# Residual kept by channel through the first two attention layers of a four-layer image kernel: one load of the image, softmax divided ahead of its transpose, no transposes ahead of the group norms

## What is computed

```python
# L0: attention over max-pooled keys, 256 tokens x 64 pooled keys
theta = x @ w_theta + b_theta;  phi, g = maxpool2x2(x @ w_phi + b_phi), maxpool2x2(x @ w_g + b_g)
x = x + sigma * (softmax(theta @ phi.T) @ g @ w_o + b_o)
# L1: group norm (32 groups), one head of 128 channels, 256 x 256 scores
n = group_norm(x) * gamma + beta
x = x + softmax(q(n) @ k(n).T / sqrt(128)) @ v(n) @ wo + bo
# L2: group norm (16 groups), 8 heads of 16 channels
x = x + concat_heads(softmax(q @ k.T / 4) @ v) @ w_out + b_out
# L3: two 2-D Hartley transforms around a block-diagonal two-layer MLP with a soft threshold
x = x + dht2d(soft_threshold(mlp(dht2d(x)))) / (16 * 128)
```

## Time and profile before

| what | value |
|---|---|
| median of 3 runs | 162.05 us (162.05 to 164.85) |
| the profiled execution, its own time | 161.73 us |
| its span, first to last instruction | 159.9 us |
| PE busy | 152.9 us, 96% of the span |
| DVE busy | 102.3 us, 64% |
| ACT busy | 106.7 us, 67% |
| POOL busy | 53.1 us, 33% |
| HBM read, written | 4.08 MB, 1.05 MB |

### The profile page before, as it was taken

The page is one execution under the profiler, slowest core; times in us unless marked ns, Lnnn a source line. Parts: engine busy times, 40 slices in busy tenths (PEclk is TensorE's granted clock), DMA queues, the critical chain, the costliest instruction groups (busy, mean ns, idle before and its releaser), DMA issues.

```text
span 159.9 us, 3806 instructions
## 1 busy us (share of the span) xinstructions
PE 152.9 (96%) x1437; PEld 117.0 (73%) x1437; DVE 102.3 (64%) x257; ACT 106.7 (67%) x245; POOL 53.1 (33%) x128
## 2 busy tenths in 40 slices
PE   7999999998999999999999999999999999999992
PEld 4787978877877767977576867567577675668992
DVE  0448778888978677658986656747685571225543
ACT  3669668757287656877357776675856778776970
POOL 6566886624802632643001125022004000024300
PEclk9999999999999999999999999999999999999999
DMA  5996000000000000000000000000002001000003
GB/s 151 239 365 264 6 2 0 2 4 0 0 0 8 0 0 4 4 0 4 0 4 6 4 0 4 3 7 0 0 3 75 0 4 37 0 4 0 21 16 131
DMA packets 3233, 5.50 MB, mean 34 GB/s; under 512 B 400, under 2 KB 2320, under 8 KB 3216
## 3 DMA queue, kind: packets, MB, share of 16 engines
q1 hardware_dynamic: 2928, 5.05, 9.5%
q10 hardware_dynamic: 288, 0.21, 0.4%
HBM read 4.08 MB, written 1.05 MB: 32 GB/s over the span
## 4 chain that ended last, share of the span: by engine, by line
PE 85%; DMA 4%; ACT 3%; DVE 2%; POOL 2%; issue 1%; SPq 1%; DVEq 0%
PE psum L692 11%; PE psum L703 10%; PE psum L671 9%; PE psum L619 5%; PE psum L599 5%; DMA tab<-in_weights 4%; PE psum L744 3%; PE psum L730 3%; PE psum L773 3%; PE psum L647 3%; PE psum L581 2%; PE psum L714 2%; PE psum L655 2%; PE psum L590 2%; PE psum L765 2%; PE psum L766 2%
## 5 line engine op out<-in xcount | busy, mean ns | idle before, releaser
L1181 DVE TENSOR_REDUCE nmax<-psum 128x4 f32<-128x1024 f32 x32 | 38.1, 1218 | 12.2 <-PE psum L671 12.1
L954 ACT ACTIVATE pT<-psum 128x1024 f32<-128x1024 f32 x32 | 31.7, 1022 | 9.1 <-PE psum L692 9.0
L692 PE MATMUL psum<-qk 32*128 32x256 f32 (+1 forms) x256 | 18.3, 400 | 0.3 <-ACT vaug_all L941 0.3
L671 PE MATMUL psum<-qk 16*128 16x256 f32 (+1 forms) x256 | 18.1, 397 | 0.3 <-ACT vaug_all L941 0.3
L703 PE MATMUL psum<-pT,vaug_all 128*32 128x256 f32 x256 | 17.1, 385 | 0.0
L365 POOL COPY zE<-zE 128x17 f32<-128x17 f32 x8 | 1.6, 199 | 40.6 <-ACT zE L970 40.6
L671 PEld LDWEIGHTS psum<-qk 16*128 16x128 f32 (+1 forms) x256 | 11.7, 184 | 4.5 <-issue 1.2
L692 PEld LDWEIGHTS psum<-qk 32*128 32x128 f32 (+1 forms) x256 | 11.6, 184 | 4.0 <-DVE nmax L1181 1.1
L429 POOL TENSOR_SCALAR nb<-nmax,e 128x1 f32<-128x1 f32 x16 | 5.8, 373 | 25.7 <-DVE nmax L1156 24.9
L359 POOL TENSOR_TENSOR rstd<-vare,half 128x1 f32<-128x1 f32 x16 | 8.8, 558 | 8.2 <-DVE vare L1139 8.1
L703 PEld LDWEIGHTS psum<-pT,vaug_all 128*32 128x32 f32 x256 | 6.7, 109 | 6.3 <-issue 2.0
(11 more groups left out here) (163 smaller groups left out, 352.7 us busy)
## 6 DMA issues: line engine op xcount, KB each, us to landing
out<-x SPq DMA_DIRECT2D x8, 128.0 KB, 2.0
tab<-in_weights SPq DMA_DIRECT2D x1, 708.0 KB, 9.5
tab<-in_weights SPq DMA_DIRECT2D x1, 640.0 KB, 5.7
x0T<-in_xT SPq DMA_DIRECT2D x4, 128.0 KB, 3.1
xin<-in_x SPq DMA_DIRECT2D x2, 256.0 KB, 7.4
x0T<-in_xT_rest SPq DMA_DIRECT2D x1, 512.0 KB, 7.7
xin<-in_x SPq DMA_DIRECT2D x1, 512.0 KB, 8.7
tab<-in_weights SPq DMA_DIRECT2D x1, 384.0 KB, 8.4
```

Of the source, the lines that this page charges most:

```text
L671: last = mm(bank[(b0, b1)[j // 2] + j % 2][:, u * TOK:(u + 1) * TOK], at[:, u, 0, :], at[:, :, 1, :], start=True, stop=True)
L692: last = mm(bank[(b0, b1)[j // 2] + j % 2][:, m * TOK:(m + 1) * TOK], at[:, m, 1, :], at[:, :, 0, :], start=True, stop=True)
L954: go(pT[g](i)[:, 2 * k:2 * k + 2].rearrange("p j m t -> p j (m t)"), pair(home["st", g, i][k]), ACT.Exp).then_inc(s["exp" + "EO"[g]], 1)
L1181: v.tensor_reduce(nmax2(i)[:, g, 2 * k:2 * k + 2, :], pair(home["sm", g, i][k]).rearrange("p j (u m) -> p j u m", u=TILES), AX.X, ALU.max, ...
```

## The change

The residual now stays by channel in `x0T` through L0 and L1, and no image by token is loaded. The steps that differ:

- `o0` and `o1` have their operands swapped, so that the output comes by channel: `o0` is two products of 128 columns (one of 258 before), `o1` two of 256 (four of 129 before). There is no column of sums any more; the division must come before the transpose, since behind it the sum of a token is spread over a row. DVE sums `p0` (`sum0_out`), takes the reciprocal, and multiplies `p0` by it in place (`p0_scaled`, 128x128). For L1, `exp1` returns the row sums itself (`accum_out`), and `p1_scaled` (128x512) divides. `p0t` and `p1t` wait for these.
- `x1_out` and `x2_out` are one instruction of 256 columns each, in place on `x0T`. `x1t` and `x1b_out` are gone. Moments and normalisation read `x0T` in SBUF instead of a transposed copy in PSUM.
- `x2t` remains, but runs late, right ahead of `ont`, into the other half of `ont`'s bank; `onc` copies both halves (512 columns instead of 256), and `x3_out` takes the residual from there. `x2b_out` writes a tile of its own.
- Two folded biases are columns of one element in place of rows of 128.
- All five lists of calls are new.

```diff
-        x0T_all, xin_all = sb("x0T", [P, IMAGES, TOK]), sb("xin", [P, IMAGES, TILES, C])
+
...
-            load_tokens(0, 2)
             load_rest()
-            load_tokens(2, 2)
-            load_tokens(4, 4)
             load_table(sp.dma_start, 3)
             load_table(sp.dma_start, 4)
...
-            def x1b_out(i, *marks):
-                after(marks)
-                if i == 0:
-                    pool.wait_ge(s["vo_rd"], 1)
-                pool.wait_ge(s["x1"], i + 1)
-                gp.tensor_tensor(x1b(i), x1(i), wide(bo1_wide[:, :]), ALU.add).then_inc(s["x1b"], 1)
-
             def x2b_out(i, *marks):
                 after(marks)
                 if i == 0:
                     pool.wait_ge(s["o2_rd"], 1)
                 pool.wait_ge(s["x2"], i + 1)
-                gp.tensor_tensor(x2b(i), x2(i), wide(b_out2[:, :]), ALU.add).then_inc(s["x2b"], 1)
+                gp.tensor_scalar(x2b(i), x0T(i), b_out2[:, :], None, ALU.add).then_inc(s["x2b"], 1)
...
-                pe.wait_ge(s["wide_b2"], 1)
-                mm(bank[b][:, 0:C], bv2_wide[:, :], w("w2_o"), start=True, stop=True).then_inc(s["fold_o2"], 1)
+                pe.wait_ge(s["b2_rd"], 1)
+                mm(bank[b][:, 0:1], w("w2_o"), bv2[:, :], start=True, stop=True).then_inc(s["fold_o2"], 1)
...
-                pe.wait_ge(s["p0"], i + 1)
+                pe.wait_ge(s["p0n"], i + 1)
...
-                mm(bank[b][:, 0:TILES * (C + 1)], p0T(i), gw_all[:, i % SLOTS].rearrange("p u c -> p (u c)"),
-                   start=True, stop=True).then_inc(s["o0"], 1)
-
-            def x1t(i, b, *marks):
-                freed(*marks)
-                home["x1t", i] = b
-                pe.wait_ge(s["x1"], i + 1)
-                for u in range(TILES):
-                    last = tr(bank[b][:, u * P:(u + 1) * P], x1(i)[:, u, :], ident)
-                last.then_inc(s["x1T"], 1)
+                for u in range(TILES):
+                    last = mm(bank[b][:, u * P:(u + 1) * P], gw_all[:, i % SLOTS, u, :], p0T(i), start=True, stop=True)
+                last.then_inc(s["o0"], 1)
...
-                mm(bank[home["x1t", i]][:, TOK:TOK + 2], w("mean1"), mv[0](i), start=True, stop=True).then_inc(s["gm1"], 1)
+                mm(bank[home["o0", i]][:, TOK:TOK + 2], w("mean1"), mv[0](i), start=True, stop=True).then_inc(s["gm1"], 1)
...
-                pe.wait_ge(s["p1"], i + 1)
+                pe.wait_ge(s["p1n"], i + 1)
...
-                for u in range(TILES):
-                    for m in range(TILES):
-                        last = mm(bank[b][:, u * (C + 1):(u + 1) * (C + 1)], p1T(i)[:, m, u * P:(u + 1) * P],
-                                  v1_all[:, i % SLOTS, m, :], start=(m == 0), stop=(m == TILES - 1))
+                for m in range(TILES):
+                    last = mm(bank[b][:, 0:TOK], v1_all[:, i % SLOTS, m, :], p1T(i)[:, m, :],
+                              start=(m == 0), stop=(m == TILES - 1))
                 last.then_inc(s["o1"], 1)
 
             def x2t(i, b, *marks):
+
                 freed(*marks)
                 home["x2t", i] = b
-                pe.wait_ge(s["x2"], i + 1)
-                for u in range(TILES):
-                    last = tr(bank[b][:, u * P:(u + 1) * P], x2(i)[:, u, :], ident)
+                pe.wait_ge(s["x2b"], i + 1)
+                for u in range(TILES):
+                    last = tr(bank[b][:, TOK + u * P:TOK + (u + 1) * P], x2b(i)[:, u * P:(u + 1) * P], ident)
...
-                    last = tr(bank[b][:, u * P:(u + 1) * P], on(i)[:, u].rearrange("p h d -> p (h d)"), ident)
+                    last = tr(bank[home["x2t", i]][:, u * P:(u + 1) * P], on(i)[:, u].rearrange("p h d -> p (h d)"), ident)
...
-                              bias=nb1(i)[:, u:u + 1])
+                              bias=nb1(i)[:, u:u + 1], accum_out=sum1(i)[:, u:u + 1])
...
-                copy(onT(i), bank[home["ont", i]][:, 0:TOK]).then_inc(s["onT"], 1)
+                copy(onT(i), bank[home["x2t", i]][:, :]).then_inc(s["onT"], 1)
...
+            def sum0_out(i, *marks):
+                after(marks)
+                dve.wait_ge(s["p0"], i + 1)
+                v.tensor_reduce(sum0(i), p0(i), AX.X, ALU.add).then_inc(s["sum0"], 1)
+
             def inv0_out(i, *marks):
                 after(marks)
+                dve.wait_ge(s["sum0"], i + 1)
+                v.reciprocal(inv0(i), sum0(i)).then_inc(s["inv0"], 1)
+
+            def p0_scaled(i, *marks):
+
+                after(marks)
+                dve.wait_ge(s["inv0"], i + 1)
+                v.tensor_tensor(p0(i), p0(i), inv0(i).unsqueeze(2).to_broadcast((P, TILES, POOLED)), ALU.mult
+                                ).then_inc(s["p0n"], 1)
+
+            def x1_out(i, *marks):
+
+                after(marks)
                 dve.wait_ge(s["o0"], i + 1)
-                sums = bank[home["o0", i]][:, 0:TILES * (C + 1)].rearrange("p (u c) -> p u c", u=TILES)[:, :, C]
-                v.reciprocal(inv0(i), sums).then_inc(s["inv0"], 1)
-
-            def x1_out(i, *marks):
-                after(marks)
-                dve.wait_ge(with_xin(i), 16)
-                dve.wait_ge(s["inv0"], i + 1)
-                for u in range(TILES):
-                    last = v.scalar_tensor_tensor(out=x1(i)[:, u, :], in0=bank[home["o0", i]][:, u * (C + 1):u * (C + 1) + C],
-                                                  scalar=inv0(i)[:, u:u + 1], in1=xin(i)[:, u, :],
-                                                  op0=ALU.mult, op1=ALU.add)
-                last.then_inc(s["x1"], 1)
+                v.tensor_tensor(x0T(i), bank[home["o0", i]][:, 0:TOK], x0T(i), ALU.add).then_inc(s["x1"], 1)
 
 
 
             def moments(i, layer, *marks):
                 after(marks)
-                dve.wait_ge(s[f"x{layer}T"], i + 1)
-                v.bn_stats(bn[layer - 1](i), bank[home[f"x{layer}t", i]][:, 0:TOK]).then_inc(s[f"bn{layer}"], 1)
+                dve.wait_ge(s[f"x{layer}"], i + 1)
+                v.bn_stats(bn[layer - 1](i), x0T(i)).then_inc(s[f"bn{layer}"], 1)
 
             def mean(i, layer, *marks):
                 after(marks)
...
-                g = bank[home[f"x{layer}t", i]][:, TOK:TOK + 2]
+                g = bank[home[f"o{layer - 1}", i]][:, TOK:TOK + 2]
...
-                x = bank[home[f"x{layer}t", i]]
-                v.tensor_scalar(xn[k](i), x[:, 0:TOK], x[:, TOK:TOK + 1], rstd[k](i), ALU.subtract, ALU.mult
+                mean_of_group = bank[home[f"o{k}", i]][:, TOK:TOK + 1]
+                v.tensor_scalar(xn[k](i), x0T(i), mean_of_group, rstd[k](i), ALU.subtract, ALU.mult
...
+                dve.wait_ge(s["p1"], i + 1)
+                v.reciprocal(inv1(i), sum1(i)).then_inc(s["inv1"], 1)
+
+            def p1_scaled(i, *marks):
+
+                after(marks)
+                dve.wait_ge(s["inv1"], i + 1)
+                v.tensor_tensor(p1(i), p1(i), inv1(i).unsqueeze(2).to_broadcast((P, TILES, TOK)), ALU.mult
+                                ).then_inc(s["p1n"], 1)
+
+            def x2_out(i, *marks):
+                after(marks)
+                if i == 0:
+                    dve.wait_ge(s["vo_rd"], 1)
+                dve.wait_ge(s["x1"], i + 1)
                 dve.wait_ge(s["o1"], i + 1)
-                sums = bank[home["o1", i]][:, 0:TILES * (C + 1)].rearrange("p (u c) -> p u c", u=TILES)[:, :, C]
-                v.reciprocal(inv1(i), sums).then_inc(s["inv1"], 1)
-
-            def x2_out(i, *marks):
-                after(marks)
-                dve.wait_ge(s["x1b"], i + 1)
-                dve.wait_ge(s["inv1"], i + 1)
-                for u in range(TILES):
-                    last = v.scalar_tensor_tensor(out=x2(i)[:, u, :], in0=bank[home["o1", i]][:, u * (C + 1):u * (C + 1) + C],
-                                                  scalar=inv1(i)[:, u:u + 1], in1=x1b(i)[:, u, :],
-                                                  op0=ALU.mult, op1=ALU.add)
-                last.then_inc(s["x2"], 1)
...
-                dve.wait_ge(s["x2b"], i + 1)
                 dve.wait_ge(s["o2"], i + 1)
-                v.tensor_tensor(x3(i).rearrange("p u c -> p (u c)"), bank[home["o2", i]][:, 0:TOK],
-                                x2b(i).rearrange("p u c -> p (u c)"), ALU.add).then_inc(s["x3"], 1)
+                v.tensor_tensor(x3(i).rearrange("p u c -> p (u c)"), bank[home["o2", i]][:, 0:TOK], onT(i)[:, TOK:2 * TOK],
+                                ALU.add).then_inc(s["x3"], 1)
 
...
-            keep_clock(11, 7); proj0(0, 0); proj0(1, 1); proj0(2, 2); proj0(3, 0, ("theta", 1))
-            s0(0, 1, ("theta", 2)); gwm(0, 3); gwm(1, 4); gwm(2, 5); s0(1, 2, ("theta", 3)); s0(2, 6); p0t(0, 1)
...
+            keep_clock(11, 7); proj0(0, 0); proj0(1, 1); proj0(2, 2); s0(0, 0); proj0(3, 3); s0(1, 1); gwm(0, 4)
+            gwm(1, 5); gwm(2, 0, ("p0", 1)); p0t(0, 2, ("theta", 3)); fold_biases(6); o0(0, 2); s0(2, 1, ("p0", 2))
```

342 lines of the change are left out of this document (161 added, 181 removed).

## The result

The kernel after took 159.53 us (median of 4, 159.26 to 159.84), against 162.05 before: a ratio of 0.985, 95% interval 0.983 to 0.987. That is 1.5% less, inside the 2% line; forecast were 158.6 and a range of 156.0 to 162.8, with more weight on faster by over 2% (0.48) than on what came (0.38).

The account below looks back on a forecast made before the run. PE, busy 96% of the span, was taken to set the time, with room on the others. The sum 161.73 - 3.2 - 0.4 + 0.3 gave 158.4, told as 158.6 us for the median; range 156.0 to 162.8.

Parts of the forecast that it names:

- PE, -3.2: PE's matmul work: 1.8 us less by `x1t`, 1.4 less by `o1`, nothing by `o0`; sum -3.2 us.
- mis-sized at 1.4: `o1` on PE: four instructions of 256 columns at 0.86 us replace 1.0 an image; 0.17 saved each, 1.4 us.
- the 1.8 of `x1t`: PE loses two transposes an image, 0.22 us, times 8: 1.8 us saved.
- The start, -0.4: Up to the first `qk1`: 1.4 us earlier, less 1.0 of moved work; 0.4 us gained, bounds 0 to 1.4.
- the group means should come near 11: At the start: image 0's group means, at 13.18 us before, should come near 11.
- What this costs PE: PE's waits from added work on DVE and ACT: +0.3 us, upper bound 3.
- DVE, +5.9 or 3.8: DVE's added work: 0.74 us an image, 5.9 in all; a faster `normalised` would take back 2.1.
- PE's share of the chain stays over 80%: Sign to check in the profile after: PE keeps over 80% of the chain of waits; it was 85%.
- the first rival: Savings fall where PE waits anyway, DVE having least room in 4 to 34 us: 161.3 or 160 us; chance 0.32.
- ACT: `onc` at 583 ns adds 1.7 us, row sums of `exp1` 2.1 taken (upper end 4.3); ACT goes to 110.5 us.
- The load and the tail: Dropping the load by token gives nothing; 4.8 us of PE work moves behind the last `pv`, not new, no term.
- the third: Rival: DVE and POOL shut each other out in divisions and `normalised`, so the kernel is slower: 167.1 us; chance 0.14.

Follow-up runs that it names:

- Experiment 1: Kernel after with two unused transposes an image put back on PE, ahead of L1's group means: 160.85 us.
- experiment 2: Kernel after without the division of L1's softmax (`p1_scaled` gone): 158.87 us, ratio 0.980 to the kernel before.
- experiment 4: Kernel after with `zsum` of image 1 ahead of two `x2b` in POOL's list: 158.41 us, ratio 0.978 to the kernel before.
- experiment 9: Kernel after with `zsum` of image 1 ahead of two `x2b` on POOL, and `x2b` as an addition of tensors: 158.85 us.
- experiment 3: Kernel after without sum, reciprocal and division of L0's softmax: 158.69 us, ratio 0.981 to the kernel before.
- experiment 11: Kernel after without L0's sums, reciprocals and divisions or L1's divisions, and with `zsum` of image 1 ahead of two `x2b`: 157.69 us.
- experiment 6: Kernel after with `exp1` without its row sums, reciprocals taken of the row maxima instead: 159.9 us.
- experiment 7: Kernel after with `exp0`'s row sums by ACT in place of DVE's eight `sum0_out`: 159.63 us, ratio 0.985 to the kernel before.
- experiment 8: Kernel after with 1 MB of unused loads back in SP's queue, where the image by token was: 159.55 us.

## Why the prediction was right, and which steps were not

- **PE, -3.2.** The sum is right, PE is busy 3.2 us less; its parts are not. `o1` is mis-sized at 1.4. The prediction set the mean of the pieces before (1.0) against the price of a product without any wait for the new ones (twice the 0.43 of `qk1`). By the pieces on the chain the means are 1.04 and 0.96, which makes 0.7 for eight images; taken for all eight from their first instruction to the one behind them, they fall from 7.95 to 7.57 us, by 0.4. The columns are hardly fewer, 8 x 129 = 1032 before and 4 x 256 = 1024 now. `x1t`, taken the same way and without the idle time recorded behind it, held PE for 2.26 us and not 1.8, and 0.2 came from `fold_out2`. The other 0.4 is spread over steps that did not change. So the 3.2 is partly luck. Experiment 1 puts back 1.3 of the 1.8 of `x1t`; no experiment puts the old `o1` back, and what the new order of calls is worth by itself was not tested.
- **The start, -0.4.** Wrong, and already by the prediction's own account: of the 1.4 its 1.0 of moved work leaves 0.4, but `x1t`'s 0.22, counted under PE, has to go too, which leaves 0.2. Measured, `qk1` is 0.45 earlier, but PE is busy only 13.22 us ahead of it where it was busy 14.20: 1.0 of work less, and 0.5 more of idle time. So the start costs 0.5, outside the bound of 0. The failed step is "the group means should come near 11". From PE's transpose of `p0` to those means the trace has 3.24 us (8.83 to 12.07), through a copy, `o0`, `x1_out`, the moments and POOL's square; so after a transpose at 8.3 or later (8.35 before the change) they could not come near 11. In the traces of experiments 2, 4 and 9, which have the same start, it is 3.2 to 3.5 us, with the means at 11.85, 12.29 and 11.70 and `qk1` at 14.90, 15.35 and 14.76. Even without sum, reciprocal and product (experiments 3 and 11) the means are at 11.58 and 11.53. From the means to `qk1` it is 3.05 us in all of them, close to the 3.2 expected. DVE's product took 0.56 in this trace and not 0.28, beside POOL's `w1n` of 0.45 that had started at 8.08; but it took 0.29 in experiment 4, where the means came later still, so this is not the cause.
- **"What this costs PE", +0.3.** Mis-sized: the page's idle time grew by 1.0, and a single wait of 1.02 behind two `x2b` is that large (experiment 4). The prediction counted POOL as rid of eight `x1b_out` and gave the new form of `x2b` no price. It is 8 x 0.2 us longer than the old one, and the new order put two of them ahead of a `zsum` that PE waits for. A list of waits that names only DVE and ACT missed the third queue.
- **DVE, +5.9 or 3.8.** Engine busy time rose by 2.5. By groups the sum is 8 x (2.17 - 1.38) = 6.3, less 16 x 0.10 for `xn` at 444 ns (between the ends 412 and 545), so 4.7. All groups together grew by 4.3; the other 1.8 is overlap, since an instruction in a row starts before the last one's end (a division of `p1` lasts 686 ns and takes 0.60 on the chain). That DVE's added work is partly bare was in the range and in the first rival. But the claim that PE's share of the chain stays over 80% was wrong (71%), and that share misleads: DVE's 20 us of the chain cost PE about 0.3 us in each of experiments 2 and 3, the rest of their 0.7 and 0.8 lies at the start and at 81 us.
- **ACT.** `onc` takes 588 ns as priced. The row sums are 3.2 us of records, but only 0.9 us of ACT's busy time by experiment 6, against 2.1 taken, and ACT is busy 108.7 us and not 110.5; neither made a difference (experiments 6 and 7).
- **The load and the tail.** Nothing each, as said (experiment 8 at full clock; 4.7 of 4.8 us).
- **The rivals.** The first was right on the place: DVE is busy 84% in 4 to 34 us, but PE kept most of its gain. Something like the lock of the third shows, and is small: `p1`'s divisions are not stretched (661 to 704 ns). The Trainium skill says (SBUF — State Buffer, "SBUF: two separate sides") that whichever of the two starts first holds the ports for its whole instruction. The trace agrees with it in two places: DVE's product 0.56 at 8.12 behind POOL's start at 8.08, and the reverse, where POOL is the one held up (below). It disagrees in others. A division of `p1` from 48.45 took 678 ns beside an `x2b` that ran from 47.92 to 48.86, and the product at 11.60 took 281 ns beside a POOL instruction from 11.56 to 12.01. So here the lock does not hold for every pair of records that overlap, and the times of POOL's records are rough.

```profile
40.98 0.94 POOL L326 TENSOR_TENSOR rstd<-vare,half 128x1 f32<-128x1 f32 x1 [1.28 <-DVE vare L1101]
```

`rstd` is 547 ns at the least and 567 in the median, and DVE's division of `p1` runs from 40.82 to 41.51.

The forecast of 158.4 from the sum is 1.1 us under the measured 159.53, and experiment 4, at 158.41, meets it. That is partly luck: 161.73 - 3.2 + 0.5 for the start is 159.0, so in experiment 4 PE's other waits shrank by 0.6 where 0.3 of growth was forecast. Which of the new order's steps shrank them was not tested.
